# Graph attention: the edge weight's term moves from a TensorE product to VectorE's pass over the fetched rows

## The chip, the cores and the metric

One Trainium2 chip, one of its NeuronCores. The metric is the device time of one execution in microseconds (us); the kernel before was run three times. Engines are named as in the profile: PE (TensorE, with PEld for its weight loads), DVE (VectorE), ACT (ScalarE), POOL (GpSimd), SP (SyncE).

## The reference

A network of four graph layers over 6250 nodes with 128 features and 200000 edges sorted by target: a sum over neighbours, a message layer with a filter, an attention layer (GATv2) and a relation layer. The change concerns the attention layer alone:

```
h  = relu(layernorm(x))
xl = h @ Wl + bl ;  xr = h @ Wr + br
e  = edge_weight1 @ We                  # [200000, 1] @ [1, 128]
m  = leaky_relu(xl[src] + xr[dst] + e, 0.2)
logits = m @ att
ex     = exp(logits - segment_max(logits, dst)[dst])
out    = segment_sum(xl[src] * (ex / (segment_sum(ex, dst)[dst] + 1e-16)), dst) + bias_out
```

The edge weight is one number for each edge, so `e` is an outer product: weight of the edge times the row `We`.

## The kernel before, in words

**Edges and pairs.** The edges lie in groups of GE = 512 (KG = 4 sets of 128, one edge on each partition; edge 4p+q lies on partition p in set q). There are NGA = 392 groups. Target nodes lie in windows of 128. One step of the edge loops treats a *pair* of a group and a window that its edges reach; a group whose edges reach two windows stands in two successive pairs. There are NG = 440 steps. Lists made on the chip say which group (`pair_group`) and window (`pair_at`, `pair_window`) a step has; an engine reads them into a register and works out from it the slot of a buffer (`slot_of`).

**The stages.** The program first packs the edges into records of four words (weight, source, target, type: `pack_edges`), then has an edge loop for each layer with some node work between: sums, filter (`filter_messages`), a sum of messages, attention (`gat_edges`), relation (`relation`). Each is a block in which all engines have a program of their own, and all meet at its end.

**The attention loop, `gat_edges`.** `skewed` writes the software pipeline: each stage of an engine has a lead, in pairs, and the engine goes through its stages in the order given for one pair after another; `turn` is the number of pairs written out in the body of the loop (S = 8, U = 4). Engines wait on counting semaphores.

- SP: `load` brings a group's records into `rows` (16 slots), `weigh_in` its weights as 9 rows of bf16 into `weight` (8 slots), and `here`, `weighed_in`, `send`, `free` pass on what has landed or is free.
- POOL: `gather` issues four indirect DMAs (L2022) for a group, which fetch 512 rows of `xl` by source into `far`. This is done for the 392 groups, not for the 440 pairs.
- DVE, in this order: `meet` (L2062, near term plus far term), `bend` (L2074, leaky ReLU), `node_max` (L2082, L2084, L2086, the running maximum), `add` (L2094), `one_hots` (L2056), `columns` (L2050, targets relative to the window), `rows_to` (L2068, copies the fetched rows of a group from `far` to one of two buffers `far_s`).
- PE, in this order: `spreads` (L2176, L2177, L2179), `sums` (L2194), `spread_keys` (L2155), `rows_met`, `turn_prob` (L2185). In `rows_met` three products of the targets' rows with the one-hot matrix (L2168) and the product of `term` with the weight rows (L2169) go to one bank, and four transposes (L2171) turn `far_s`.
- ACT: copies out of PSUM (L2112, L2107, L2124), the exponentials (L2129, L2132), and L2118 and L2141.

The weight rows come from three bf16 parts: POOL splits the weights in `pack_edges` (`split_weights`), SP stores nine rows to memory (`store_weights`, L300) and waits for them at the end of the block (L351), and at the head of `gat_edges` DVE splits `We` likewise (L235 to L239) and builds `term` (L2035 to L2039), after it has cleared `weight` (L2032).

Of the kernel before, what the change touches and what calls it, by code (L numbers as in the profile page):

```python
# [12 lines left out]
BF16 = mybir.dt.bfloat16  # L13
# [66 lines left out]
def program(nc, x, src, dst, attr, etype, weight, W1, b1, W2, b2, W_in, W_f1, b_f1, W_f2, b_f2,  # L80
# [16 lines left out]
    with top:  # L97
# [7 lines left out]
        wrows = dram("weight_rows", [9, 2 * EP], BF16)  # L105
# [46 lines left out]
        def link(eng, ins):  # L152
# [11 lines left out]
        k.pair_lists, k.pair_bases, k.softs, k.wrows, k.gtable = pair_lists, pair_bases, softs, wrows, gtable  # L164
# [31 lines left out]
            "records_in", "weights_here", "rows_here", "rows_free", "weights_zeroed", "far_here", "far_taken", "marked", "product_ready", "message_turned")}  # L196
# [45 lines left out]
def pack_edges(k, kept):  # L242
# [17 lines left out]
    with ExitStack() as own:  # L260
# [3 lines left out]
        wt_rest = sb(own, "wt_rest", [P, J])  # L264
        wt_parts = [k.staging_t[:, :].bitcast(BF16)[:, 0:J], *(sb(own, f"wt_part{i}", [P, J], BF16) for i in (1, 2))]
# [19 lines left out]
        wt_split, wt_out = sem("wt_split"), sem("wt_out")  # L285

        def split_weights(eng, done):

            nc_eng = nc.gpsimd
            nc_eng.tensor_copy(wt_parts[0][:, :], e_wt[:, :]).then_inc(wt_split, 1)  # L290
            eng.wait_ge(wt_split, done + 1)
            nc_eng.tensor_tensor(wt_rest[:, :], e_wt[:, :], wt_parts[0][:, :], ALU.subtract).then_inc(wt_split, 1)
            eng.wait_ge(wt_split, done + 2)
            nc_eng.tensor_copy(wt_parts[1][:, :], wt_rest[:, :]).then_inc(wt_split, 1)
            eng.wait_ge(wt_split, done + 3)
            nc_eng.tensor_tensor(wt_parts[2][:, :], wt_rest[:, :], wt_parts[1][:, :], ALU.subtract).then_inc(wt_split, 1)

        def store_weights(eng, half):
            for r in range(9):
                eng.dma_start(k.wrows[r, half * EP:(half + 1) * EP].rearrange("(p j) -> p j", p=P), wt_parts[r % 3][:, :])\  # L300
                    .then_inc(wt_out, 16)
# [17 lines left out]
        with nc.Block() as block:  # L319
            @block.sync  # L320
            def _(sp):
# [25 lines left out]
                sp.wait_ge(wt_split, 4)  # L347
                store_weights(sp, 0)
                sp.wait_ge(rec_out, 48)
                sp.wait_ge(row_out, 16 * (NB + 1))  # L350
                sp.wait_ge(wt_out, 9 * 16)  # L351

            @block.gpsimd
            def _(pool):
# [25 lines left out]
                split_weights(pool, 0)  # L380
# [160 lines left out]
        earlier, owned, attr_out, wt_back, wt_free = sem("earlier"), sem("owned"), sem("attr_out"), sem("wt_back"), sem("wt_free")  # L541
# [5 lines left out]
        with nc.Block() as block:  # L547
# [43 lines left out]
            def _(sp):  # L591
                with if_mixed(sp):
# [18 lines left out]
                    with sp.Fori(0, NCH, 1) as c:  # L611
                        sp.wait_ge(wt_free, c + 1)
                        sp.dma_start(part[:, :, :].rearrange("p t c -> p (t c)"),
                                     k.erec[EP:2 * EP, :].rearrange("(p j) c -> p (j c)", p=P)[:, bass.ds(c * (T * RW), T * RW)])\
                            .then_inc(wt_back, 16)
                    sp.wait_ge(wt_split, 8)
                    store_weights(sp, 1)
                    sp.wait_ge(wt_out, 18 * 16)

            @block.gpsimd  # L620
            def _(pool):
                with if_mixed(pool):
# [12 lines left out]
                    pool.sem_inc(moved, 1)  # L635
                    pool.sem_inc(wt_free, 1)
                    with pool.Fori(0, NCH, 1) as c:
                        pool.wait_ge(wt_back, c * 16 + 16)
                        nc.gpsimd.tensor_copy(e_wt[:, bass.ds(c * T, T)], part[:, :, C_WT]).then_inc(wt_free, 1)
                    pool.wait_ge(wt_free, NCH + 1)  # L640
                    split_weights(pool, 4)


def scan(k, dve, source, n):

    cur, other = source, 0
    step = 1
# [1283 lines left out]
def gat_edges(k):  # L1931
# [16 lines left out]
    with ExitStack() as own:  # L1948
# [28 lines left out]
        with nc.Block() as block:  # L1977
            @block.sync
            def _(sp):
# [9 lines left out]
                def weigh_in(g, a):  # L1989
                    if isinstance(g, int) and a == 0:  # L1990
                        sp.wait_ge(k.stage["weights_zeroed"], 1)
# [753 lines left out]
```

## Time and profile before

| | us |
|---|---|
| median of three runs | 9282.66 (9282.63 to 9282.89) |
| profiled execution, its own time | 9295.66 |
| its span, first to last instruction | 9294.0 |
| PE busy (80% of the span) | 7420.9 |
| DVE busy (67%) | 6266.4 |
| POOL busy (67%) | 6250.4 |
| ACT busy (54%) | 5033.5 |
| attention loop, first to last L2084 | 4917.9 to 6993.3 |

The busy shares are means over stages with different limits. What the change is worth has to be read in the attention loop, at the head of it, and where the packing ends. A DVE instruction is shown with its start and its duration; durations of neighbours can overlap by some tens of nanoseconds, so the time that one takes in a row is the distance from start to start. "issue" is idle time of an engine in which the profile shows nothing that it waited for: its sequencer was at work on registers, addresses and waits.

### The profile page before, as it was taken

Reading aid. Unit: us, or ns where it says so; the run is one execution under the profiler, and the core shown is the slowest. Engines: PE = TensorE matmul, PEld = TensorE weight load, DVE = VectorE, ACT = ScalarE, POOL = GpSimd, SP = SyncE. Lnnn points to the kernel's source line nnn. Section 1 sums busy time; section 2 is a strip of 40 time slices with the busy share of each in tenths; the row PEclk is TensorE's granted clock in tenths of the full one; section 3 lists DMA queues with packets and bytes.
Section 4 is the critical chain, followed back from the end, with each engine's and each line's share of the span. In section 5 each row is a group of like instructions: output and inputs, shape, how many; then the busy total and the mean of one; then the engine's idle time right before and its main releaser. Section 6 shows DMA issues by size and latency. Waiting matters only on the chain. (4 is left out here: it accounts for less than half of the span.)

```text
span 9294.0 us, 257139 instructions
## 1 busy us (share of the span) xinstructions
PE 7420.9 (80%) x48775; PEld 5025.9 (54%) x49109; DVE 6266.4 (67%) x20821; ACT 5033.5 (54%) x11808; POOL 6250.4 (67%) x6542
## 2 busy tenths in 40 slices
PE   3699999996666666666978999999995777777777
PEld 2344455554333333335965666666663666666666
DVE  6577777776444455557976777777777666666666
ACT  4366666664333333332334555666665666666666
POOL 4777777772777777774217777777763766766664
PEclk7555555557888888888989999999998999999999
DMA  6355555553333344446842222222221222222221
GB/s 191 103 143 144 147 148 150 150 150 98 107 109 110 113 113 116 115 117 189 262 124 55 56 55 55 54 53 54 52 45 38 54 51 51 51 51 50 51 51 48
DMA packets 1004337, 900.19 MB, mean 97 GB/s; under 512 B 689602, under 2 KB 748099, under 8 KB 1003590
## 3 DMA queue, kind: packets, MB, share of 16 engines
q0 software_dynamic: 243504, 526.87, 21.2%
q10 hardware_dynamic: 309878, 260.87, 9.9%
q1 hardware_dynamic: 450592, 109.24, 5.4%
q14 instruction: 334, 2.74, 0.1%
q8 instruction: 29, 0.48, 0.0%
HBM read 663.38 MB, written 248.90 MB: 98 GB/s over the span
## 5 line engine op out<-in xcount | busy, mean ns | idle before, releaser
L2022 POOL DMA_INDIRECT a_far<-attention_table,a_rows x1568 | 1548.2, 987 | 657.9 <-issue 489.2
L1769 POOL DMA_INDIRECT message_records<-hs,f_pos x1564 | 1522.1, 973 | 622.9 <-issue 438.2
L2278 POOL DMA_INDIRECT r_far<-node_table,r_rows x1568 | 1488.7, 949 | 636.1 <-issue 452.2
L1377 POOL DMA_INDIRECT near<-split_table,t_rows x1568 | 1518.4, 968 | 482.1 <-issue 476.9
L1859 ACT ACTIVATE hs<-banks,f_rows 128x128 f32 x1760 | 503.1, 368 | 1200.6 <-DVE hs L1819 1084.5
L1565 PE MATMUL banks<-near,w_f 20*128 20x512 f32 x784 | 807.6, 1130 | 26.5 <-DVE list_store L1453 25.1
L1556 PE MATMUL banks<-near,t_hot 128*128 x5292 | 694.8, 304 | 167.0 <-SPq L1352 106.9
L1556 PEld LDWEIGHTS banks<-near,t_hot 128*128 128x128 bf16 x5292 | 586.1, 135 | 313.0 <-issue 228.3
L2129 ACT ACTIVATE list_store<-banks,staging 128x512 f32<-128x512 f32 x442 | 303.9, 688 | 819.6 <-DVE staging L2086 817.6
L1900 PE MATMUL banks<-f_hot_t,near 128*128 128x512 bf16 x1218 | 420.4, 458 | 357.3 <-DVE f_hot_t L1797 348.1
L1818 DVE COPY hs<-f_rows 128x12 int32 x441 | 84.7, 192 | 887.7 <-SPq L1753 884.6
L2417 PE MATMUL banks<-near,r_hot_t 128*128 x5328 | 621.7, 232 | 39.2 <-issue 1.9
L2194 PEld LDWEIGHTS banks<-a_far,a_prob 128*128 128x128 f32 x3528 | 431.1, 190 | 276.6 <-issue 276.6
L1904 PE MATMUL banks<-list_store,w_W_f 128*128 128x512 f32 x886 | 559.2, 719 | 0.0
L1890 PEld LDWEIGHTS banks<-ident_b,f_rel 128*128 128x128 bf16 x1780 | 131.4, 107 | 754.2 <-DVE f_rel L1791 648.2
L1462 DVE SCALAR_TENSOR_TENSOR near<-list_store,xs 128x512 f32<-128x512 f32 x392 | 268.3, 684 | 394.3 <-ACT xs L1514 374.4
L2444 PE MATMUL banks<-r_far,list_store 128*128 x3528 | 531.6, 296 | 0.0
L2382 ACT ACTIVATE list_store<-banks,r_prob 128x128 f32<-128x128 bf16 x1764 | 498.3, 364 | 40.0 <-PE banks L2428 27.3
L1573 PEld LDWEIGHTS banks<-ident,t_attr 128*20 128x20 f32 x1568 | 156.0, 120 | 642.2 <-issue 587.2
L2417 PEld LDWEIGHTS banks<-near,r_hot_t 128*128 128x128 bf16 x5328 | 432.2, 103 | 120.9 <-issue 98.3
L1679 PE MATMUL banks<-m_rows,m_hot 128*128 128x128 f32 x3528 | 434.9, 281 | 65.5 <-DVE m_hot L1640 45.6
L2194 PE MATMUL banks<-a_far,a_prob 128*128 x3528 | 476.3, 277 | 8.9 <-issue 3.9
(445 smaller groups left out, 19688.3 us busy)
## 6 DMA issues: line engine op xcount, KB each, us to landing
list_store<-soft_groups ACTq DMA_DIRECT2D x447, 256.0 KB
soft_groups<-near ACTq DMA_DIRECT2D x392, 256.0 KB
m_rows<-message_records SPq DMA_DIRECT2D x223, 264.0 KB
m_rows<-message_records POOLq DMA_DIRECT2D x223, 264.0 KB
near<-split_table,t_rows POOLq DMA_INDIRECT x1568
a_far<-attention_table,a_rows POOLq DMA_INDIRECT x1568
r_far<-node_table,r_rows POOLq DMA_INDIRECT x1568
message_records<-hs,f_pos POOLq DMA_INDIRECT x1564
```

What stands on the lines that cost most here:

```text
L1377: pool.indirect_dma_start(far[:, u * KG + q, :], None, k.table3[:, :], bass.IndirectOffsetOnAxis(ap=rows[:, u, q, C_SRC:C_SRC + 1].bitcast ...
L1556: last = nc.tensor.matmul(k.psum[a % 2][:, 0:D], hot[:, a % H, q, :], row[:, part * D:(part + 1) * D], start=q == 0 and part == 0, stop=q ...
L1565: nc.tensor.matmul(hidden_ps[a % 2], k.w_f1[:, :], attr_t[:, a % 2, :], start=True, stop=True).then_inc(hidden_ready, 1)
L1769: pool.indirect_dma_start(k.mrec[:, :], bass.IndirectOffsetOnAxis(ap=pos[:, u, q:q + 1], axis=0), msg[:, u * KG + q, :], None)\
L1859: last = nc.scalar.activation(msg[:, bass.ds(slot + q, 1), 0:D].rearrange("p a d -> p (a d)"), out_ps[b][:, q * D:(q + 1) * D], ACT.Copy, ...
L1904: nc.tensor.matmul(filter_ps[b], w_f2[:, :], soft[:, s, :], start=True, stop=True).then_inc(filter_ready, 1)
L2022: pool.indirect_dma_start(far[:, u, q, :], None, k.gtable[:, :], bass.IndirectOffsetOnAxis(ap=rows[:, a % R, q, C_SRC:C_SRC + 1].bitcast(I ...
L2194: last = nc.tensor.matmul(sum_ps[b][:, 0:D + 1], prob[:, b, q * P:(q + 1) * P], flat(far[:, slot, q, 0:D + 1]), start=q == 0, stop=q == KG ...
L2278: pool.indirect_dma_start(far[:, u, q, 0:D], None, k.table[:, :], bass.IndirectOffsetOnAxis(ap=rows[:, a % R, q, M_DST - M_SRC:M_DST - M_S ...
L2382: last = nc.scalar.activation(share[:, b, q, :], hot_ps[:, q * P:(q + 1) * P], ACT.Copy, scale=prob[:, u, q:q + 1])
L2417: nc.tensor.matmul(near_ps[b][:, span], hot_t[:, h, span], k.near[:, w, part * D:(part + 1) * D] .rearrange("p a d -> p (a d)"), start=par ...
L2444: last = nc.tensor.matmul(sum_ps[b][:, 0:D + 1], share[:, b, q, :], flat(far[:, slot, q, 0:D + 1]), start=q == 0, stop=q == KG - 1)
```

## The change

What it does, part by part:

1. `rows_to` no longer copies a group's 512 fetched rows with one instruction. It does four `scalar_tensor_tensor`, one for each set of 128: `far_s[q] = We * weight of the edge + far[q]`, where the weight is read from the record in `rows` by a pointer to one number for each partition. It therefore needs two slots, that in `far` (of 8) and that in `rows` (of 16).
2. PE's product L2169 goes, with its wait for `weights_here` and its slot.
3. SP's `weigh_in` and `weighed_in` go from the loop; `weight`, its clearing, `term`, `split3` of `We` and `which` go from the head of `gat_edges`.
4. `split_weights` and `store_weights` go from both blocks of `pack_edges` (the second runs only where the edges aren't sorted), with the wait for the stores.
5. The body of DVE's loop holds 4 pairs and not 8 (`turn=U`), and `rel` has 4 slots. PE and ACT keep 8.

```
-                sp.wait_ge(wt_split, 4)
-                store_weights(sp, 0)
                 sp.wait_ge(rec_out, 48)
                 sp.wait_ge(row_out, 16 * (NB + 1))
-                sp.wait_ge(wt_out, 9 * 16)
...
-                split_weights(pool, 0)
...
-                skewed(sp, (FREE, free), (LOAD, load), (HERE, here), (WEIGHT, weigh_in), (WEIGHED, weighed_in), (SENT, send), counts=now, turn=R, total=NGA, exact=True)
+                skewed(sp, (FREE, free), (LOAD, load), (HERE, here), (SENT, send), counts=now, turn=R, total=NGA, exact=True)
...
-                nc.vector.memset(weight[:, :, :], 0.0).then_inc(k.stage["weights_zeroed"], 1)
-                nc.vector.tensor_scalar(att[:, :], k.ones[:, :], k.att_col[:, :], None, ALU.mult)
-                split3(nc, link, split[0][:, :], split[1][:, :], split[2][:, :], We[:, :], left[:, :])
-                link(nc.vector.tensor_tensor(which[:, 0:3], k.ident[:, 0:9:3], k.ident[:, 1:9:3], ALU.add))
-                link(nc.vector.tensor_tensor(which[:, 0:3], which[:, 0:3], k.ident[:, 2:9:3], ALU.add))
-                link(nc.vector.tensor_scalar(term[:, :], split[0][:, :], which[:, 0:1], None, ALU.mult))
-                for i in (1, 2):
-                    link(nc.vector.scalar_tensor_tensor(term[:, :], split[i][:, :], which[:, i:i + 1], term[:, :], ALU.mult, ALU.add))
+                link(nc.vector.tensor_scalar(att[:, :], k.ones[:, :], k.att_col[:, :], None, ALU.mult))
...
                     wait(dve, now, near_ready, g, a, 2)
-                    nc.vector.tensor_copy(far_s[a % 2], far[:, bass.ds(slot_of(group), 1), :, 0:D].rearrange("p a q d -> p (a q) d"))\
-                        .then_inc(far_here, 1)
+                    slot, held = bass.ds(slot_of(group), 1), bass.ds(slot_of(group, R), 1)
+                    for q in range(KG):
+                        last = nc.vector.scalar_tensor_tensor(far_s[a % 2][:, q, :], We[:, :], flat(rows[:, held, q, C_WT:C_WT + 1]),
+                                                              flat(far[:, slot, q, 0:D]), ALU.mult, ALU.add)
+                    last.then_inc(far_here, 1)
...
-                skewed(dve, (SCORE, meet), (SCORE, bend), (MAX, node_max), (ADD, add), (HOT, one_hots), (COLS, columns), (HOT, rows_to), counts=now, turn=S)
+                skewed(dve, (SCORE, meet), (SCORE, bend), (MAX, node_max), (ADD, add), (HOT, one_hots), (COLS, columns), (HOT, rows_to), counts=now, turn=U)
...
-                    pe.wait_ge(weights_here, group)
                     wait(pe, now, far_here, g, a)
                     wait(pe, now, in1, g, a, 1)
                     wait(pe, now, onehotT_ready, g, a)
                     for i in range(3):
-                        nc.tensor.matmul(near_ps, flat(k.near[:, w, i * D:(i + 1) * D]), hot_t[:, a % H, :], start=i == 0, stop=False)
-                    nc.tensor.matmul(near_ps, term[:, :], weight[:, slot, :].rearrange("p a (e q) -> p (a q) e", q=KG), start=False, stop=True)
+                        nc.tensor.matmul(near_ps, flat(k.near[:, w, i * D:(i + 1) * D]), hot_t[:, a % H, :], start=i == 0, stop=i == 2)
```

## Rows read from the trace of the kernel before

**Rows 1.** The page: busy time of each engine over the span.
```profile
PE 7420.9 (80%) x48775; PEld 5025.9 (54%) x49109; DVE 6266.4 (67%) x20821; ACT 5033.5 (54%) x11808; POOL 6250.4 (67%) x6542
```

**Rows 2.** Stretches: attention early and late, filter; busy us, clock, DMA, GB/s.
```profile
core 0: us, PE busy (x) PEld busy (x) DVE busy (x) ACT busy (x) POOL busy (x), PEclk, DMA share, GB/s
4950.00:5320.00 370.00, 349.22 (x2075) 231.32 (x2112) 260.32 (x681) 206.05 (x526) 280.34 (x295) 1.00 0.26 56
6210.00:6580.00 370.00, 355.01 (x2200) 246.73 (x2240) 280.76 (x720) 226.00 (x559) 283.32 (x280) 1.00 0.25 53
2500.00:4200.00 1700.00, 1097.28 (x4819) 574.08 (x4911) 867.46 (x2268) 624.20 (x1890) 1294.12 (x1331) 0.85 0.40 113
```

**Rows 3.** One line's instructions: DVE's reduction (one a pair), POOL's gathers.
```profile
L2084 DVE TENSOR_REDUCE a_gmax<-banks x442: 672/679/684, 4917.9 to 6993.3; 128x1 f32<-128x512 f32 x148
```
```profile
L2022 POOL DMA_INDIRECT a_far<-attention_table,a_rows x1568: 941/947/1465, 4893.0 to 6947.4; - x196
```

**Rows 4.** Groups of 6210 to 6580 (80 pairs): busy, mean ns, idle before.
```profile
L2169 PE MATMUL banks<-a_weight,staging_t 128*128 x80 | 49.1, 614 | 0.0
...
L2062 DVE TENSOR_TENSOR staging_t<-banks,staging_t 128x512 f32<-128x512 f32 x80 | 55.3, 692 | 4.8
...
L2050 DVE TENSOR_SCALAR a_rel<-a_rows,list_store 128x4 f32 x80 | 20.1, 252 | 35.3 <-issue 32.2 <-SPq L1997 3.1
L2068 DVE COPY list_store<-a_far 128x512 f32 x40 | 17.4, 435 | 21.3 <-PE banks L2171 21.3
...
L2169 PEld LDWEIGHTS banks<-a_weight,staging_t 128*128 128x128 bf16 x80 | 7.6, 95 | 18.3 <-issue 18.3
```

**Rows 5.** Timeline of DVE, one pair of the attention loop: start, us.
```profile
6301.84 0.69 DVE L2062 TENSOR_TENSOR staging_t<-banks,staging_t 128x512 f32<-128x512 f32 x1
...
6304.40 0.35 DVE L2056 TENSOR_SCALAR a_hot_t<-a_keys,part_id 128x512 bf16<-128x512 bf16 x1
6305.17 0.23 DVE L2050 TENSOR_SCALAR a_rel<-a_rows,list_store 128x4 f32 x1 [0.43 <-issue]
6305.94 0.43 DVE L2068 COPY a_far_s<-a_far 128x512 f32 x1 [0.54 <-PE banks L2171]
6306.45 0.69 DVE L2062 TENSOR_TENSOR staging_t<-banks,staging_t 128x512 f32<-128x512 f32 x1
```

**Rows 6.** Timeline of DVE at the beginning of the attention loop.
```profile
4908.31 0.23 DVE L2050 TENSOR_SCALAR a_rel<-a_rows,list_store 128x4 f32 x1
4909.08 0.43 DVE L2068 COPY a_far_s<-a_far 128x512 f32 x1 [0.54 <-issue]
```

**Rows 7.** Timeline of DVE elsewhere: four, then two, short instructions in a row.
```profile
7011.24 1.12 DVE L2476 SCALAR_TENSOR_TENSOR hs<-acc,stat,hs 128x128 f32<-128x128 f32 x4
```
```profile
8006.20 0.29 DVE L2318 SCALAR_TENSOR_TENSOR r_work<-banks,r_far 128x128 f32<-128x128 f32 x1
...
8006.41 0.29 DVE L2318 SCALAR_TENSOR_TENSOR r_work<-banks,r_far 128x128 f32<-128x128 f32 x1
```

**Rows 8.** Timeline of DVE where a loop turns: attention, then relation.
```profile
6217.93 0.43 DVE L2068 COPY list_store<-a_far 128x512 f32 x1 [0.56 <-PE banks L2171]
6218.50 0.69 DVE L2062 TENSOR_TENSOR staging_t<-banks,staging_t 128x512 f32<-128x512 f32 x1
```
```profile
8017.35 0.35 DVE L2306 TENSOR_SCALAR r_hot_t<-r_keys,part_id 128x512 bf16<-128x512 bf16 x1 [3.65 <-PE banks L2428]
```

**Rows 9.** End of the first packing block: DVE's last instruction, SP's wait, SP's last stores.
```profile
114.61 0.21 DVE L530 TENSOR_TENSOR first<-scan,count 128x50 f32<-128x50 f32 x1
```
```profile
SPq L351 <- DMA weight_rows<-wt_part: 4.0, 1, 4.0
```
```profile
116.04 2.00 SPq L300 DMA_DIRECT2D weight_rows<-wt_part  x2
```

**Rows 10.** Timeline of DVE at the head of the attention block.
```profile
4890.04 1.76 DVE L2032 MEMSET a_weight<- 128x2048 uint32 x1 [1.68 <-PEq L1121]
...
4896.30 5.56 DVE L2040 MEMSET acc<- 128x6600 f32 x1 [1.44 <-issue]
```

More of the change, by code:

```diff
@@ L1943, in gat_edges @@
     wait, start = stages.wait, stages.start
-    records_in, rows_here, rows_free, weights_here = (k.stage[n] for n in ("records_in", "rows_here", "rows_free", "weights_here"))
+    records_in, rows_here, rows_free = (k.stage[n] for n in ("records_in", "rows_here", "rows_free"))
     We = k.wide["We"][0]
@@ L1949, in gat_edges @@
         sb = lambda name, shape, dt=F32: k.sb(own, "a_" + name, shape, dt)
-        rows, rel = sb("rows", [P, R, KG, RW]), sb("rel", [P, S, KG])
-        weight = sb("weight", [P, S, GE], BF16)
+        rows, rel = sb("rows", [P, R, KG, RW]), sb("rel", [P, U, KG])
         keys, hot_t = sb("keys", [P, 2, GE], BF16), sb("hot_t", [P, H, GE], BF16)
@@ L1955, in gat_edges @@
         prob_t = spare[:, GE:3 * GE].rearrange("p (b c) -> p b c", b=2)
-        att, term, left, *split = (k.staging_t[:, i * D:(i + 1) * D] for i in range(6))
-        term, split = term.bitcast(BF16)[:, 0:D], [t.bitcast(BF16)[:, 0:D] for t in split]
+        att = k.staging_t[:, 0:D]
         far_t = k.staging_t[:, 2 * D:6 * D]
         far_s = [t.rearrange("p (q d) -> p q d", d=D) for t in (spare[:, 0:GE], sb("far_s", [P, GE]))]
-        leaky, which = sb("leaky", [P, 2, GE]), sb("which", [P, 3])
+        leaky = sb("leaky", [P, 2, GE])
         gmax, before, bounded, factor = sb("gmax", [P, 1]), sb("before", [P, U]), sb("bounded", [P, U]), sb("factor", [P, U])
@@ L1967, in gat_edges @@
         flat = lambda t: t.rearrange("p a c -> p (a c)")
-        s_load, s_gather = [k.since(x) for x in loads_in], [k.since(x) for x in gathered]
+        s_gather = [k.since(x) for x in gathered]
         def slot_count(now, g, a, each, base=0):
@@ L1987, in load @@
                         .then_inc(k.rows_in[a % U], 16)
-                def weigh_in(g, a):
-                    if isinstance(g, int) and a == 0:
-                        sp.wait_ge(k.stage["weights_zeroed"], 1)
-                    u = a % S
-                    sp.dma_start(weight[0:9, u, :], k.wrows[:, bass.ds(moved + (g + a) * GE, GE)]).then_inc(loads_in[u], 16)
                 def here(g, a):
@@ L1997, in here @@
                     sp.sem_inc(records_in, 1)
-                def weighed_in(g, a):
-                    sp.wait_ge(loads_in[a % S], slot_count(now, g, a, 16, s_load[a % S]))
-                    sp.sem_inc(weights_here, 1)
                 def send(g, a):
@@ L2159, in rows_met @@
                 def rows_met(g, a):
-                    pair = pair_at(pe, k, o, g + a)
-                    w, group = window_in(k, pair), group_in(pair)
-                    slot = bass.ds(slot_of(group), 1)
-                    pe.wait_ge(weights_here, group)
+                    w = pair_window(pe, k, o, g + a)
                     wait(pe, now, far_here, g, a)
@@ L2199, in gat_edges @@
     for u in range(S):
-        k.since.passed(16 * len(range(u, NGA, S)), loads_in[u])
         k.since.passed(16 * KG * len(range(u, NGA, S)), gathered[u])
```

45 lines of the change are left out of this document (7 added, 38 removed).

## The prediction

> **What bounds the kernel now.** I read the page first. Its shares [rows 1] make PE look like the limit, at 80% of the span, with DVE and POOL both at 67%. They are means over stages, so I went to the stretches of the attention loop. There PE is busy 355.01 of 370 us late in the loop [rows 2], which still points to PE; but the late stretch holds 80 pairs, so a pair takes 370 / 80 = 4.625 us, and the question is how much of that each engine needs.
>
> The groups and the timeline of DVE answer for DVE. It is busy 280.76 / 80 = 3.51 us a pair [rows 2], which leaves 1.11 idle. Nearly all of that lies ahead of two short instructions: 35.3 / 80 = 0.44 before L2050 and 21.3 / 40 = 0.53 before L2068 [rows 4]. The first is called issue. The second is put down to PE's transposes L2171; the reader is to see that it isn't theirs. The distance from L2050's start to L2068's is 0.77 us in the running loop [rows 5], and also 0.77 at the loop's beginning, where the same gap of 0.54 is called issue [rows 6]. Both instructions follow a read of the list (`pair_group`) into a register, and each starts 0.77 after the one ahead of it. So this is the sequencer's own work, which the next instruction can't overlap. The only true slack of DVE is the 4.8 / 80 = 0.06 us ahead of L2062 [rows 4]. From L2062's start to L2068's there are 6305.94 - 6301.84 = 4.10 us [rows 5], and with the copy's 0.43 DVE can't go below 4.53 a pair. PE and DVE are both at the limit.
>
> POOL is the third. In the early stretch it issued 295 gathers in 370 us [rows 2], 1.254 us each or 5.02 for a group, and there it holds the pairs back; its 1568 gathers need 1966 us at least, and took 2054 [rows 3]. The loop took 6993.3 - 4917.9 = 2075.4 us from the first to the last L2084, over 441 distances [rows 3], 4.706 a pair. Late in the loop groups reach into two windows more often, pairs are more than groups, and PE and DVE rule.
>
> **The change, part by part.**
>
> *Four products in place of the copy.* The nearest rows: four `scalar_tensor_tensor` of 128x128 with a pointer scalar and all operands in SBUF take 1.12 us together [rows 7], and the last one's tail overlaps what follows it. In the relation loop a like instruction without a pointer, whose input also has a slot from a register, is 0.29 long and starts 0.21 after its neighbour [rows 7], so the tail is about 0.08, and one in the row costs (1.12 - 0.08) / 4 = 0.26. Lower end 0.21, upper end 1.12 / 4 = 0.28. I take 0.26, since that row has the pointer and the change has it too: four cost 1.04, where the copy took 0.43.
>
> *The second slot.* Ahead of the first product the sequencer works out one more slot, in `rows`. DVE shows no such step alone; PE does: its load for L2169 is preceded by 18.3 / 80 = 0.23 us of issue [rows 4], which is a slot and its address. I take 0.23, with 0 (hidden) and 0.46 (twice, as each of the four has two addresses) as ends.
>
> *The shorter body.* Where the attention loop turns, L2062 starts 0.57 after L2068 [rows 8]; behind the last product it would otherwise start after 0.26. The 0.31 is paid once in 4 pairs, 0.08 a pair. Today most of it hides in the copy's 0.43 and the slack, once in 8 pairs.
>
> *DVE's pace.* 4.10 + 0.23 + 1.04 + 0.08 = 5.45 us a pair. Nothing covers it: DVE had 0.06 of slack, and 5.45 is above POOL's 5.02 for a group too, so it holds in the early part as well, and with all pairs. The loop becomes 441 x 5.45 = 2403.5 us, 328.1 more. Ends: 4.10 + 0 + 0.84 + 0.08 = 5.02, and 4.10 + 0.46 + 1.12 + 0.08 = 5.76.
>
> A rule of the Trainium skill bears on the price of the four products. By "VectorE: DVE Perf Modes", section "The TRN2 errata", an SBUF-to-SBUF instruction of VectorE takes 58 cycles plus its elements at 0.96 GHz, so splitting a tile pays the fixed part each time, which speaks against this change. An estimate from it is 4 x 186 / 0.96 = 0.78 us, a pace of 5.19, and 9485 us. Rows 7 show more, 0.26 against 0.19 for each.
>
> *PE's product gone.* 49.1 / 80 = 0.61 us busy a pair and the 0.23 of issue [rows 4] go. It is worth nothing: PE would need about 4.2 of the 5.45, and waits for DVE. The transposes then wait for the products to end, some 0.8 later within DVE's turn than now, and the sum L2062 for that pair is a whole turn away, so this stays covered; if the cover were gone it would show as a gap ahead of L2062.
>
> *SP.* Two of its six stages go, with a DMA a group. SP isn't late in the loop: worth nothing.
>
> *Head of the attention block.* From the clearing of `weight` to that of `acc` there are 6.26 us [rows 10]; 0.2 for `att` and the 1.44 of issue ahead of `acc` stay, 4.6 go. All on DVE, which is now first to be late; ends 0 and 6.3.
>
> *End of the packing.* DVE is done at 114.8; SP's last two stores of weight rows are out at 118.0 and it waits 4.0 more for them to land [rows 9]. All engines meet there, so up to 118.0 + 4.0 - 114.8 = 7.2 us go. Other stores may still be landing, so I take 6.0, ends 0 and 7.2. POOL's split runs under DVE's work and is worth nothing.
>
> **The sum.** + 328.1 - 4.6 - 6.0 = + 317.5. The profiled execution took 9295.66 with a span of 9294.0, and becomes 9613; the median of the runs lies 13 lower, at 9282.66, so I say 9282.7 + 317.5 = 9600. DVE's two ends of pace give 9410 and 9737. What a measurement of this kernel can tell from no change is about 0.2%, 19 us.
>
> **The rivals.**
>
> *DVE's gap is a wait after all, and the products fill it (faster).* If the 0.53 ahead of L2068 waited for PE or for rows, as the view of groups says, losing L2169 would shorten it and the products would run where DVE now stands still. DVE would need 3.51 - 0.43 + 1.04 + 0.44 = 4.56 a pair in place of 4.625, 0.065 x 441 = 28 us, with the 10.6 of head and packing 9244; POOL's floor of 1966 allows no more than 88 + 10.6, 9184. The point that decides is a mean pace of 4.706 + 10.6 / 441 = 4.73. Against it stands the same 0.77 with nothing to wait for [rows 6]. Chance 0.07; 0.02 more that it lands within 0.2%.
>
> *The turn of the loop stalls.* In the relation loop DVE stands still 3.65 us once in eight pairs [rows 8], at the turn. Were that so here, once in four, a pair would cost 3.65 / 4 = 0.91 more: 6.36, and 10001 us. Against it: the attention loop of 8 pairs with 9 instructions of DVE each, 72, turns in 0.57, and the new body has 4 x 12 = 48. The Trainium skill, "Runtime: NRT & Kernel Launch", section "Instruction fetch mechanics", says that a branch to code which isn't held on the engine has to fetch it; by that rule the shorter body is what keeps the stall away. Chance 0.03.
>
> *PE's clock falls.* It is at 1.00 now; in the filter stage, with PE busy 1097.28 of 1700 us, 65%, it is 0.85 [rows 2], which is 1.2 GHz in 30% of the time. Here PE would be busy (355.01 / 80 - 0.61) / 5.45 = 70%. At 1.2 GHz its 3.83 us of work could double to 7.7, above DVE's pace, and 0.3 x (7.7 - 5.45) = 0.67 more a pair gives 6.12 and 9896. Against it: PE's idle time would come in short pieces, some 1.6 us in every pair. Chance 0.08.
>
> **How the numbers follow.** The forecast, DVE's pace between 5.0 and 5.8, has 0.80. The predicted time is its own, 9600. Its middle part, slot and pitch not at their ends together, is a pace of 5.18 to 5.76, 9480 to 9740; I leave out the low end, the faster rival and most of the two slow ones, together about 0.2. Faster 0.07, within 0.2% 0.02, slower 0.80 + 0.03 + 0.08 = 0.91.
>
> **What would show it right or wrong.** Right: in the attention loop four products start about 0.26 apart, the first some 1.0 after L2050's counterpart; no gap ahead of the sum; L2084's counterparts are 5.4 to 5.5 apart from first to last, early and late alike; POOL waits for free slots from early on; DVE's busy share in the loop is near (3.51 - 0.43 + 1.2) / 5.45 = 79%, PE's near 70%; the first gather of the program starts 6 us earlier. Wrong: pairs 4.6 or 5.0 apart (DVE hid the products, or POOL paces), a gap of some us once in four pairs, or a clock below 0.95 in the loop. The weakest term is the sequencer's: if each product waits for two addresses, all four cost more than 0.28; if the slot hides, the pace is nearer 5.2.

## The result, and the profile after

The changed kernel took 9567.72 us, the median of 4 runs (9563.87 to 9569.29), and the kernel before 9282.65, the median of 4 (9281.87 to 9282.89). The ratio is 1.0307, with a 95% interval of 1.0294 to 1.0320: slower by 285 us. Forecast were 9600 us, +317.5, in a range of 9480 to 9740, with 0.91 for slower. Mechanism and sign were right; the sum was 32 us too high, 9 of them in the loop that the change is in and 23 outside it.

From here DVE's old lines L2050, L2062, L2068 and L2084 are L1993, L2005, L2013 (four products where the copy was) and L2030, the gathers L2022 are L1972, and L505, L511 and L512 of the packing are L481, L487 and L488. First the page and the stretches of the kernel after, which answer to [rows 1, 2]:

```profile
PE 7373.3 (77%) x48331; PEld 4966.8 (52%) x48665; DVE 6539.4 (68%) x22145; ACT 4984.8 (52%) x11808; POOL 6214.0 (65%) x6538
```
```profile
4950.00:5320.00 370.00, 300.19 (x1805) 200.93 (x1840) 281.05 (x818) 185.07 (x479) 287.10 (x273) 1.00 0.23 50
6210.00:6580.00 370.00, 300.50 (x1807) 201.09 (x1842) 281.03 (x818) 185.02 (x480) 220.95 (x232) 1.00 0.20 43
```

The early and the late stretch are now alike in DVE, PE and ScalarE, which they were not before: one engine sets the pace throughout. Each stretch of 370 us holds 68 pairs (818 instructions of DVE, 12 a pair). DVE is busy only 76% of it, since a good part of what limits it is not busy time. PE's share is 81%, where 70% was forecast, and its clock is 1.00, so the rival with the falling clock is out.

The view of a line, after, answers to [rows 3]:

```profile
L2030 DVE TENSOR_REDUCE a_gmax<-banks x442: 677/680/691, 4889.4 to 7283.8; 128x1 f32<-128x512 f32 x148
```
```profile
L1972 POOL DMA_INDIRECT a_far<-attention_table,a_rows x1568: 938/944/1345, 4869.6 to 7228.1; - x196
```

From the first to the last reduction there are 7283.8 - 4889.4 = 2394.4 us, 319.0 more than before and 2394.4 / 441 = 5.43 a pair; 5.45 was forecast.

DVE's timeline, one pair, answers to [rows 5]:

```profile
6304.82 0.68 DVE L2005 TENSOR_TENSOR staging_t<-banks,staging_t 128x512 f32<-128x512 f32 x1
6305.54 0.69 DVE L2020 SCALAR_TENSOR_TENSOR a_leaky<-staging_t 128x512 f32<-128x512 f32 x1
...
6307.38 0.35 DVE L1999 TENSOR_SCALAR a_hot_t<-a_keys,part_id 128x512 bf16<-128x512 bf16 x1
6308.16 0.23 DVE L1993 TENSOR_SCALAR a_rel<-a_rows,list_store 128x4 f32 x1 [0.44 <-issue]
6309.16 1.14 DVE L2013 SCALAR_TENSOR_TENSOR list_store<-wide_We,a_rows,a_far 128x128 f32<-128x128 f32 x4 [0.76 <-issue]
6310.23 0.69 DVE L2005 TENSOR_TENSOR staging_t<-banks,staging_t 128x512 f32<-128x512 f32 x1
```

The reader is to see three things. From L2005 to the first product there are 6309.16 - 6304.82 = 4.34 us, where the sum had 4.10 + 0.23. The four products are 1.14 long together, with the next instruction 1.07 behind their start. And nothing stands ahead of L2005: both idle times of the pair are called issue, as are all but 4.7 us of those ahead of the two lines over the whole loop.

In the packing, DVE's count of the keys, L528 before and L504 after, moved by more than the forecast allowed:

```profile
112.52 0.21 DVE L528 COPY count<-banks 128x50 f32<-128x50 f32 x1 [0.75 <-PE banks L431]
```
```profile
103.43 0.21 DVE L504 COPY count<-banks 128x50 f32<-128x50 f32 x1 [0.75 <-PE banks L407]
```

DVE itself was done 9.1 us sooner. Nothing in the forecast had DVE's own work there get shorter. With DVE out of the way, the block now ends with SP, which waits for its last stores of the table's rows, issued up to 109.99:

```profile
SPq L328 <- DMA split_table<-near: 2.3, 1, 2.3
```

### The profile page after: what moved, and what is told of

The parts are those of the page before. It is cut to its first block and busy times, and to the rows that moved or that the text cites. A ratio compares the mean times of both kernels' runs of the same rounds, so it can differ in the third digit from the quotient of the medians.

```text
span 9567.3 us, 256120 instructions
## 1 busy us (share of the span) xinstructions
PE 7373.3 (77%) x48331; PEld 4966.8 (52%) x48665; DVE 6539.4 (68%) x22145; ACT 4984.8 (52%) x11808; POOL 6214.0 (65%) x6538
## 5 line engine op out<-in xcount | busy, mean ns | idle before, releaser
L1972 POOL DMA_INDIRECT a_far<-attention_table,a_rows x1568 | 1537.2, 980 | 973.4 <-issue 519.3
L1518 PE MATMUL banks<-near,t_hot 128*128 x5292 | 692.8, 305 | 164.1 <-SPq L1314 105.7
L2136 PE MATMUL banks<-a_far,a_prob 128*128 x3528 | 509.3, 287 | 79.4 <-issue 79.3
L2127 PE MATMUL banks<-ident,list_store 128*128 128x128 f32 x1768 | 290.3, 287 | 348.0 <-ACT list_store L2075 348.0
L2259 DVE SCALAR_TENSOR_TENSOR r_work<-banks,r_far 128x128 f32<-128x128 f32 x1772 | 413.9, 287 | 132.1 <-issue 99.8
```

Source lines behind the costliest of these rows:

```text
L1518: last = nc.tensor.matmul(k.psum[a % 2][:, 0:D], hot[:, a % H, q, :], row[:, part * D:(part + 1) * D], start=q == 0 and part == 0, stop=q ...
L1972: pool.indirect_dma_start(far[:, u, q, :], None, k.gtable[:, :], bass.IndirectOffsetOnAxis(ap=rows[:, a % R, q, C_SRC:C_SRC + 1].bitcast(I ...
L2136: last = nc.tensor.matmul(sum_ps[b][:, 0:D + 1], prob[:, b, q * P:(q + 1) * P], flat(far[:, slot, q, 0:D + 1]), start=q == 0, stop=q == KG ...
```

## The experiments

Twelve kernels ran. Seven stood beside runs of the kernel before with medians of 9280.3 us (the first four) and 9277.8 us (the last three):

| kernel | us, median | ratio to before, 95% | attention loop, us | relation loop, us |
|---|---|---|---|---|
| before | 9282.65 | | 2075.4 | 2133.2 |
| after | 9567.72 | 1.0294 to 1.0320 | 2394.4 | 2115.6 |
| e1_turn8 | 9639.91 | 1.0374 to 1.0409 | 2390.0 | 2192.8 |
| e2_before_turn4 | 9221.85 | 0.9923 to 0.9956 | 2071.3 | 2075.3 |
| e3_fixed_pointer | 9464.21 | 1.0182 to 1.0217 | 2317.1 | 2092.9 |
| e4_copy_no_term | 9227.25 | 0.9928 to 0.9961 | 2071.6 | 2099.7 |
| e10_order3 | 9307.41 | 1.0019 to 1.0042 | 2135.3 | 2116.9 |
| e11_order3_relation4 | 9160.28 | 0.9856 to 0.9889 | 2134.4 | 1967.2 |
| e12_before_both | 9161.62 | 0.9857 to 0.9889 | 2121.8 | 1969.1 |

The loops are the distances from the first to the last of 442 maxima over a pair, a_gmax and r_gmax, in the view of that line. The other five (e5, e6, e7, e9, e13) ran on another chip, called chip 8 below, where the four edge loops with POOL's indirect transfers took 25 to 46% longer and the kernel before 12174 to 12176 us. The sum of messages, a loop without such transfers, and the packing took what they did before (452.6 us for 451.9 from the first to the last L1602, in e9 and after). Something else than DVE's work sets the pace there: e5 and e6, which are the changed kernel but for a part of the packing, took 12196.85 and 12202.74 us against 12176.2, 0.2% more in place of 3.1%. So only durations, order and waits on an engine are read from these five.

**The four products and their slots.** Two kernels take the product's parts off one by one. e3 gives the four products a pointer that stands in a fixed place, so that no second slot is worked out (it leaves out the edge's weight and multiplies the row by the partition's number):

```
- flat(rows[:, held, q, C_WT:C_WT + 1])
+ k.part_id[:, 0:1]
```


> The changed kernel whose four products read their pointer scalar from a fixed column (the partition's number) and not from the record, so the slot in the records isn't worked out; it leaves out the edge weight and multiplies the row by that column. Theory, the slot is sequencer work ahead of the first product: the pace falls from 5.43 by 0.22 to 5.21 and the time by 97 us to 9470; the four products stay 0.26 apart. Rival, the slot is hidden or the products' own two addresses are the limit: the distance from the relative targets to the first product stays 1.0, or the products come closer together.

e4 has the old copy instead, and leaves the term out altogether, on PE as well:

```
- for q in range(KG): ... scalar_tensor_tensor(far_s[a % 2][:, q, :], We, ...)
+ nc.vector.tensor_copy(far_s[a % 2], far[:, slot, :, 0:D].rearrange(...))
```


> The changed kernel with the copy in place of the four products, and nothing of the edge weight's term on any engine: it leaves the term out. Theory, DVE sets the pace: without PE's product DVE needs 4.10 + 0.43 + 0.04 for the turn = 4.57 a pair late in the loop against 4.625 before, POOL 5.02 for a group early; 14 us less than before in the loop and 28 to 45 less outside it: 9225 to 9242. PE shows idle time in the late part. Rival, PE's product was what set the late pace, and DVE would follow: a late pace of 4.2 to 4.4 and about 9190.

Both came within 6 us of what was expected, e3 at 9464 for 9470 and e4 at 9227 for 9225 to 9242. The second slot is worth (2394.4 - 2317.1) / 441 = 0.18 us a pair, the products against the copy (2317.1 - 2071.6) / 441 = 0.56 over the loop. The latter is a mean that POOL holds down: early in e4's loop the gathers pace it, as before. e4 also says what PE's product for the term had cost: its loop is 2071.6 us and that of e2, which has the product, 2071.3. Nothing, as forecast. And DVE's two gaps stay with PE's product gone, as e4's timeline shows:

```profile
6305.19 0.23 DVE L1993 TENSOR_SCALAR a_rel<-a_rows,list_store 128x4 f32 x1 [0.43 <-issue]
6306.06 0.43 DVE L2012 COPY a_far_s<-a_far 128x512 f32 x1 [0.64 <-issue]
```

That it is sequencer work shows in the view of the line, where register operations stand as DVEq. Before, then after:

```profile
L2068 DVEq ALU_OP  x890: 45/45/45, 4907.2 to 6995.8; - x178
L2068 DVEq FUSED_REGOPS  x445: 57/57/65, 4907.4 to 6995.8; - x149
```
```profile
L2013 DVEq FUSED_REGOPS  x2225: 57/93/117, 4879.0 to 7287.0; - x186
L2013 DVEq ALU_OP  x1335: 40/45/45, 4878.8 to 7286.5; - x191
...
  issue: 349.7, 441
```

The 445 pairs had two operations and a fused one ahead of the copy. Now they have three and five fused. One more operation, of 0.04 us, and one more fused one, of 0.07 in the pair shown, stand ahead of the first product; from the first of these operations to DVE's instruction the trace has 0.25 us in the pair of [rows 5] and 0.47 now. The other three fused ones go with the products behind it, whose distance stayed at 0.26. The last row is DVE's idle time ahead of L2013 that nothing but issue ends: 0.79 us a pair.

**Does the length of DVE's body matter?** Two kernels change it alone, the attention loop's of the changed kernel back to eight pairs, and that of the kernel before to four:

```
- skewed(dve, ..., (HOT, rows_to), counts=now, turn=U)    # after: 4
+ skewed(dve, ..., (HOT, rows_to), counts=now, turn=S)    # e1: 8, e2 the other way
```


> The changed kernel with DVE's body written out for eight pairs again (and eight slots of the relative targets). Theory, DVE's own work sets the pace of 5.43 us and a turn costs 0.31 us: paid once in eight pairs, it saves 0.04 a pair, 17 us, so about 9550, pace 5.39. Rival, a body this long stalls at its turn as the relation loop's does (3.65 us before): about 0.4 a pair more, 9720 to 9740, with one gap of 3 to 4 us in every eight pairs ahead of DVE's sum of near and far term. The body has 96 DVE instructions, between the 72 that turned without a stall and the relation loop's 168, so I hold both for equally likely.

> The kernel before with DVE's body of four pairs and nothing else of the change. Theory: the shorter body costs a turn (0.57 in place of at most 0.51 from the copy to the sum) once in four pairs and not in eight, at most 0.03 a pair and only late in the loop where DVE and PE set the pace: 9283 to 9292. Rival, the 285 us come from the shorter body and not from the products: 9500 or more.

In the attention loop the body's length is worth 2394.4 - 2390.0 = 4.4 us and 2075.4 - 2071.3 = 4.1 us: neither a stall nor a gain. Once in four against once in eight was to cost 0.04 a pair, half of the forecast's 0.08, and costs 0.01. Both times moved all the same, and neither lies where it was expected, e1's by 72 us up and e2's by 58 down, and that happened in the relation loop, whose source neither touches: 77 us longer and 58 shorter. Its DVE stands still once in eight pairs, at the turn [rows 8], and by how much differs from build to build. After and e1, timeline of DVE there:

```profile
8033.74 0.35 DVE L2247 TENSOR_SCALAR r_hot_t<-r_keys,part_id 128x512 bf16<-128x512 bf16 x1 [2.96 <-ACT r_keys L2301]
```
```profile
8008.30 0.35 DVE L2247 TENSOR_SCALAR r_hot_t<-r_keys,part_id 128x512 bf16<-128x512 bf16 x1 [3.14 <-ACT r_keys L2301]
...
8010.41 0.35 DVE L2288 SCALAR_TENSOR_TENSOR r_cur<-r_cur,r_factor,banks 128x129 f32<-128x129 f32 x1 [1.48 <-issue]
```

The second kernel has a second standstill, of 1.48 us, right behind the first; it comes in 51 of the 55 turns and makes 77 us. In the seven kernels of the table whose relation loop has eight pairs, the interval with the turn lasts from 7.5 (e2) to 9.5 us (e1) on average and every other one 4.1 to 4.7.

**The relation loop's turn.** e9 and e11 give that loop a body of four pairs, with its rings cut from eight slots to four:

```
- u, f = a % S, bass.ds(g + a, 1)          # and likewise in each ring
+ u, f = a % U, bass.ds(g + a, 1)
- skewed(dve, ..., (COLS, columns), counts=now, turn=S)
+ skewed(dve, ..., (COLS, columns), counts=now, turn=U)
```


> The changed kernel with VectorE's relation loop turned every four pairs and not every eight (its rings cut from eight slots to four; nothing is left out); the attention loop is untouched. It measures what the once-per-turn standstill of the relation loop is worth, which moved by itself between the kernels so far (relation loop 2136 us before, 2118 after, 2078 and 2196 in the two runs with another body length in the attention loop). Theory (the loop's first instructions have to be fetched again when the body is long, as in the relation loop's 8 pairs, and not when it is short): intervals of 4.1 to 4.7 us throughout and no 8.1 us one, relation loop 1880 to 1960 us, time 9330 to 9410 us. Rival (a standstill of the same size comes at each turn, so twice as often): relation loop 2300 us or more, time over 9750 us. Second rival (the shorter rings make VectorE wait for TensorE): no standstill, but intervals over 4.8 us, time 9500 to 9600 us.

e9 fell on chip 8 (12205.13 us against 12176.2) and decides nothing. e11, below, repeats it on top of e10: relation loop 2116.9 to 1967.2, time 9307.41 to 9160.28, 7 and 10 us above the ranges expected. In the whole loop DVE has no idle time over 1.3 us left, where e10 has 56. So the long body pays about 2.7 us a turn, net, and the short one nothing of the kind. Body and rings were shortened together, and no run has one without the other. The Trainium skill, "Runtime: NRT & Kernel Launch", section "Instruction fetch mechanics", says that a branch back to code outside the stretch held on the engine waits for a fetch. The runs agree in that the two attention bodies, of four and of eight pairs, turn freely and the longer relation body doesn't; what moves the amount from build to build wasn't tried by itself, so that it is the code's place is only argued.

**The packing.** Each of the two parts that the change removed from the packing was put back alone, POOL's four split instructions (e5) and nine stores of the same size by SP, of a tile that is there anyway (e6). The tiles have 128x1570 elements, not the 128x785 that the two expectations say:

```
+ nc.gpsimd.tensor_copy(wt_parts[0][:, :], e_wt[:, :]) ... # e5, and three more on POOL
```
```
+ for r in range(9):                                        # e6
+     sp.dma_start(k.wrows[r, 0:EP]..., win[0][:, :]).then_inc(wt_out, 16)
+ sp.wait_ge(wt_out, 9 * 16)
```


> The changed kernel with one removed part put back: POOL splits the 128x785 weights in three in the first packing block (its four instructions, nothing stored). Theory: POOL's instructions on large tiles slow VectorE's instructions that run at the same time, so VectorE's cast on L511's line goes from 0.43 to about 1.6 us, the subtraction after it from 0.69 to about 3.5 us, and the packing block ends 6 to 9 us later; the first gather of relation-free stages moves from 121.7 to 128 to 131 us, and the time from 9568 to 9574 to 9577 us. Rival, the prediction's own term (POOL's split is hidden and worth nothing): VectorE's durations stay 0.43 and 0.69 us, first gather 121.7 to 122.5, time 9568 us within the noise of the relation loop (20 us).

> The changed kernel with the other removed part of the packing block put back: nine stores of one tile of 128x785 bf16 into a table that nobody reads, issued by SP at the end of the first packing block, with the wait for them; nothing is split. Prediction's term: stores and their wait end the block 6.0 us later, first gather at 127.7 us. Theory after the traces: SP's stores run beside VectorE's and SP's other work, VectorE's end sets the block's, and the stores alone cost 0.5 to 2 us: first gather at 122 to 124 us. Either way the time stays within 9560 to 9580 us, so the verdict is read from the start of the first gather, not from the time.

Timeline of DVE with the split (before, one line, then e5), then without (after); POOL's first two split instructions in e5 are the last fence:

```profile
55.17 3.52 DVE L512 TENSOR_TENSOR near<-x_rest,near 128x512 bf16<-128x512 f32 x1
```
```profile
53.37 1.60 DVE L497 CAST near<-x_rest 128x512 bf16<-128x512 f32 x1
55.01 3.52 DVE L498 TENSOR_TENSOR near<-x_rest,near 128x512 bf16<-128x512 f32 x1
58.45 1.85 DVE L491 TENSOR_SCALAR win_halves<-win_halves 128x1570 bf16<-128x1570 bf16 x1
```
```profile
53.44 0.43 DVE L487 CAST near<-x_rest 128x512 bf16<-128x512 f32 x1
53.91 0.69 DVE L488 TENSOR_TENSOR near<-x_rest,near 128x512 bf16<-128x512 f32 x1
54.51 1.04 DVE L481 TENSOR_SCALAR win_halves<-win_halves 128x1570 bf16<-128x1570 bf16 x2
```
```profile
52.74 1.95 POOL L360 CAST staging_t<-e_wt 128x1570 bf16<-128x1570 f32 x1
54.78 3.20 POOL L362 TENSOR_TENSOR wt_rest<-e_wt,staging_t 128x1570 f32<-128x1570 f32 x1
```

A cast of 0.43 us takes 1.60 and a subtraction of 0.69 takes 3.52: each ends 0.3 to 0.6 us after the POOL instruction that runs beside it (54.97 against 54.69, 58.53 against 57.98). DVE isn't slowed in proportion, it is held until POOL has finished. With the split DVE's count came at 112.08, without it (e9, same chip) at 103.49. The Trainium skill says this in "SBUF — State Buffer", section "SBUF: two separate sides": the port pair that VectorE and GpSimd share is a lock, which an instruction that needs it (of VectorE: one in a two-port mode, or with two inputs in SBUF) has until it ends. The two durations agree with that. By that rule the forecast should have priced the split.

The stores, alone, left DVE where it was (count at 103.55) and held the block's end: SP waited 4.7 us for them, and POOL's first gather came at 129.32 us against 120.35 in e9, 9.0 later. My expectation of 0.5 to 2 us was wrong. The split, alone, moved DVE's count by 8.6 us but the first gather only to 123.77, 3.4 later, where I had expected 6 to 9: without the stores the block ends with whichever is later, DVE (done at 114.4 in e5) or SP's stores of rows (landed at 109.99 + 2.3 = 112.3 in the changed kernel). So the two parts overlap. In the kernel before the stores of weights, landed at 122.0, covered DVE's 114.8; with the stores alone gone DVE would be the end, 7.2 us sooner, and only with the split gone too does the end move the last 2.5. One start is good to some us only: in the nine kernels of the table the first gather comes at 129.2 to 131.0 with both parts and at 119.2 to 122.1 without, and e7, with e9's packing, began at 125.49, its count 4.7 us late as well.

**The order of DVE's stages.** If a slot costs what the instruction ahead of it doesn't cover, a long instruction ahead of it should hide it. e7 puts the products behind the sum:

```
- (SCORE, meet), (SCORE, bend), (MAX, node_max), (ADD, add), (HOT, one_hots), (COLS, columns), (HOT, rows_to)
+ (SCORE, meet), (HOT, rows_to), (SCORE, bend), (COLS, columns), (MAX, node_max), (ADD, add), (HOT, one_hots)
```


> The changed kernel with VectorE's stages in another order: the sum with the near rows, then the four products, then the leaky step, the keys' subtraction, the running maximum, the addition and the one-hot test. Nothing is left out. Theory (what a pair costs on VectorE is not its 4.3 us of busy time but the idle 0.77 and 0.75 us in which its sequencer loads and computes two register slots behind short instructions): with the register work behind the 0.65 us sum and the 0.6 us leaky step, the pace falls from 5.43 to 4.6 to 4.9 us, the loop by 230 to 365 us, the time to 9200 to 9340 us. Rival (the pair is bound by the length of VectorE's instructions or by the chain through TensorE, and the order is immaterial): pace 5.35 to 5.5 us, 9540 to 9600 us. Second rival (the products in front wait for the gathered rows or for TensorE's turning of the pair before): VectorE's idle time in front of the products ends in a semaphore, pace over 5.5 us.

e7 fell on chip 8 as well (12164.21 against 12176.2 us), but its DVE timeline answers, in a stretch where no transfer was late:

```profile
8002.90 0.69 DVE L2005 TENSOR_TENSOR staging_t<-banks,staging_t 128x512 f32<-128x512 f32 x1 [1.55 <-ACT staging_t L2058]
8003.98 1.14 DVE L2013 SCALAR_TENSOR_TENSOR list_store<-wide_We,a_rows,a_far 128x128 f32<-128x128 f32 x4 [0.38 <-issue]
8005.03 0.68 DVE L2020 SCALAR_TENSOR_TENSOR a_leaky<-staging_t 128x512 f32<-128x512 f32 x1
8005.64 0.22 DVE L1993 TENSOR_SCALAR a_rel<-a_rows,list_store 128x4 f32 x1
...
8006.61 0.16 DVE L2032 SCALAR_TENSOR_TENSOR staging<-a_gmax,a_bounded 128x1 f32<-128x1 f32 x1
...
8008.88 0.69 DVE L2005 TENSOR_TENSOR staging_t<-banks,staging_t 128x512 f32<-128x512 f32 x1 [1.53 <-ACT staging_t L2058]
```

The gap ahead of the products fell from 0.76 to 0.38 and that ahead of L1993 went. But the pair grew to 8008.88 - 8002.90 = 5.98 us: from the start of L2032, whose end lets ScalarE go on, DVE has only 0.7 us of work left before the next sum, and ScalarE needs 2.2 until its copy for that sum is there. It was the wait that took the gap's place. In this loop 278 of 442 pairs are 5.9 to 6.1 us apart and none less than 5.7; in e9, with the old order on the same chip, the commonest are 5.4 and 5.5. The 4.6 to 4.9 expected didn't come. e10 keeps the products in that place and moves only the keys' subtraction behind the sum and the one-hot test behind the products:

```
+ (SCORE, meet), (COLS, columns), (SCORE, bend), (MAX, node_max), (ADD, add), (HOT, rows_to), (HOT, one_hots)
```


> The changed kernel with VectorE's attention stages in a third order: the sum with the near rows, the keys' subtraction, the leaky step, the running maximum, the addition, the four products, the one-hot test. Nothing is left out. The order with the products straight behind the sum (e7_order) closed the idle time ahead of them from 0.75 to 0.38 us and ahead of the keys' subtraction from 0.38 to nothing, but put only 0.8 us of work between the maximum's last step and the next sum, while ScalarE's four instructions after that step and its copy of the far rows take 2.2 us, so VectorE then waited 1.5 us for ScalarE. Here the four products (idle time and all 1.7 us) stand in that place again. Theory (a slot's register work costs what the instruction ahead of it doesn't cover): keys' subtraction covered by the 0.69 us sum, products 0.65 us behind the 0.35 us addition: 0.70 + 0.13 + 0.60 + 0.12 + 0.72 + 0.13 + 0.98 + 1.05 + 0.35 = 4.8 us a pair, the loop 280 us shorter than the changed kernel's, the time 9270 to 9310 us on a chip that gives the kernel before 9283 us. Rival (register work costs its 1 us wherever it stands): 5.3 to 5.45 us a pair, 9510 to 9575 us. Second rival (VectorE waits for ScalarE here too): idle time in front of the sum, ended by ScalarE, pace over 5 us.

9307.41 us, in the range expected and 260 less than the changed kernel, for the same instructions. DVE's idle time ahead of L1993 and L2013, views of the two lines, after and then e10:

```profile
  issue: 194.2, 442
```
```profile
  issue: 2.2, 3
  SPq L1951: 0.5, 1
```
```profile
  PE banks L2113: 215.4, 316
  SPq L1955: 77.6, 78
  issue: 35.1, 51
```

The 194.2 us ahead of the keys' subtraction are gone; ahead of the products 349.7 + 3.3 became 215.4 + 77.6 + 35.1 = 328.1, since the 0.35 us addition covers little. The name PE is again that of whatever came last by the profile: with it as with issue the gap is 0.6 to 0.8 us nearly each time. The 78 under SPq L1955, which passes on that gathered rows have landed, are 1.0 us in the median and lie mostly in the early half; there POOL's gathers hold DVE in part.

**Both kernels at their best.** e11 is e10 with the relation loop's short body. e12 is the kernel before with short bodies in both loops and e10's order, the copy where e10 has the products:

> e10_order3 with VectorE's relation loop turned every four pairs (rings of four). Nothing is left out. Against e10_order3 it gives the relation loop's once-per-turn standstill alone, on a chip whose DMA is not the limit. Theory (a long body has to be fetched again at its turn, a short one doesn't): no interval of 8 us left, relation loop 1880 to 1960 us instead of 2080 to 2200, time 9040 to 9150 us. Rival (a standstill at each turn, twice as often): relation loop over 2300 us, 9500 us or more. Second rival (rings of four make VectorE wait for TensorE): intervals over 4.8 us throughout, time about that of e10_order3.

> The kernel before with the same three things: attention body of four pairs, VectorE's stages in e10_order3's order (its copy of the fetched rows in the place of the four products), relation body of four pairs. TensorE's product for the weight, the weight rows and their loads are all in. It tells what the change itself is worth once VectorE's register work is covered. Theory (the copy's slot is loaded behind the addition, the keys' subtraction is covered, TensorE at some 4.3 us a pair comes next): attention pace 4.3 to 4.5 us against 4.63, time 8900 to 9000 us, still 150 us or more ahead of e11_order3_relation4, because 1.05 us of products stand against a copy of 0.37 us. Rival (without the weight's product on TensorE the changed kernel is the faster of the two): over 9100 us.

They took 9160.28 and 9161.62 us, both 1.3% ahead of the kernel before and over 400 us ahead of the changed one, and the change is worth nothing between them: 12.6 us more in the attention loop, and 14 less outside it. I expected e12 to take 8900 to 9000 us and to lead by 150. It doesn't, because in it the copy is too short for the place, as the view of its L2062 shows:

```profile
L2062 DVE TENSOR_TENSOR staging_t<-banks,staging_t x443: 670/691/694, 4897.6 to 7023.9; 128x512 f32<-128x512 f32 x148
its engine sat idle before it (us, times) until:
  ACT staging_t L2112: 210.7, 374
```

The sum waits 210.7 us in all, 0.48 a pair, for ScalarE's copy, where e10's products fill the time: 2121.8 against 2134.4 us of loop. e12's order made its loop 50 us longer than the 2071.3 of e2. The last kernel was to give the kernel before its own order and both short bodies:

```
- skewed(dve, (HOT, one_hots), ..., (COLS, columns), counts=now, turn=S)   # relation, e2 plus e9's edit
+ skewed(dve, (HOT, one_hots), ..., (COLS, columns), counts=now, turn=U)
```


> The kernel before with its own order of VectorE's attention stages, and both of VectorE's bodies of four pairs (attention and relation). Nothing is left out and TensorE's product for the weight is in. It tells whether the change is worth anything when each kernel has the order that suits it: e11_order3_relation4, the changed kernel at its best, took 9160 us. Theory (in the kernel before the order was not what was short: 4.63 us a pair in e2_before_turn4 against 4.77 in e12_before_both, where the sum waited 0.5 us for ScalarE): attention loop 2071 us, relation loop 1970 us, so 9222 less 2078 plus 1970: 9105 to 9125 us, some 45 us ahead of e11. Rival (the relation loop's gain belongs to the attention loop's other order, by where the code comes to lie): relation loop over 2050 us, 9190 us or more.

It fell on chip 8, 12196.94 against 12174.39 us. Whether the kernel before, at its best, is ahead of e11 stays open; 9221.85 - 2075.3 + 1968 = 9115 would be the estimate.

## Why the prediction was right, point by point

- **What bounds the loop.** Right. DVE's chain of starts sets the pair, and the two gaps, which the groups put down to PE's transposes in part [rows 4], are the sequencer's. e4 and the two orders show it from two sides: with PE's product gone both stay (0.43 and 0.64 us); with a longer instruction ahead the first goes (e7, e10) and the second halves (0.76 to 0.38 in e7).
- **Four products.** Forecast 4 x 0.26 = 1.04; measured 1.05 to 1.07 to the next start. The 0.78 that the lower estimate had for the four, and its 9485 us, didn't come.
- **The second slot.** Forecast 0.23, from a row of PE's; measured 0.24 by distance (4.34 against 4.10) and 0.18 by leaving it out.
- **The turn.** 0.08 forecast; the half of it that e1 can tell, 0.04, measured 0.01. This term was too high and the products' a little too low, so that 5.45 for 5.43 is in part luck.
- **The loop.** +328.1 forecast, +319.0 measured.
- **PE's product and SP's stages worth nothing.** Right, by e4 against e2, and with PE's clock at 1.00. But PE is busy 300.50 / 68.2 = 4.41 us a pair and not 3.83, hence the 81%: the product's 0.61 can't be taken off a busy time of 4.44 in which records overlap. The rival with the clock was worked out from the 3.83; at 4.41 its loss would have been larger.
- **Head of the block.** -4.6 forecast. The first gather of the stage came 4893.0 - 4869.6 = 23.4 us sooner and the first reduction 4917.9 - 4889.4 = 28.5, so the head gave 5.1; against e2, which has the old head, it gave 4.6.
- **The packing.** The step that failed is "POOL's split runs under DVE's work and is worth nothing". It held DVE for 8.6 us, and the 7.2 us that the forecast took as the most that could go were counted to DVE's old end, 114.8. DVE ended at 105.7, SP's stores of rows became the end, and the block's first gather came 131.04 - 121.67 = 9.4 us sooner, not 6.0.
- **What the sum had no term for.** Outside the loop the profiled executions differ by 273.3 - 319.0 = -45.7 us, where -10.6 was forecast: 9.4 in the packing, 14.0 from there to the attention stage's first gather, 5.1 in the head, and 17.2 behind the loop, all of that in the relation loop (2133.2 to 2115.6), by a smaller standstill at its turns, which by the second experiment is a thing of the build. The 14.0 are hardly the change's: the execution profiled of before lay 13.0 above its median, that of after 1.6, and e2, with before's code up to there, reached the attention loop's first reduction 12.3 us sooner than it, at 4905.6. Against e2 the changed kernel is 4905.6 - 4889.4 = 16.2 us sooner there, and 319.0 - 16.2 - 17.6 = 285.2 us is what the medians say too (285.1). By this count the 32 us that the forecast was too high are 9 in the attention loop, 6 in packing and head and 18 in the relation loop, where it had no term.
- **The rivals.** None came: no wait that the products filled, no stall at the attention loop's turn, no fall of the clock. POOL waits for free slots from early on: 273 gathers in the early stretch in place of 295 [rows 2], and 303.0 us of waiting ahead of its gathers in place of 17.6.

## What to carry to other kernels

Where an engine's idle time is called issue ahead of a short instruction with an address from a register, price the register work as a span from the start of the instruction ahead, here some 1.0 us for two slots and 0.77 for one, and put a long instruction there; it was worth 260 us here, nearly the whole loss of the change. But before moving stages, count what the order leaves between the instruction that frees the next engine and the one that needs its answer: ScalarE's 2.2 us made the pairs of e7's better-looking order longer than those of the one it replaced. And when a time moves, look first whether the moved time lies in the loop that was edited.

## What the runs showed of the hardware that I had not expected

- DVE is held, not slowed, beside POOL's large instructions: 0.69 us became 3.52 beside one of 3.20. How much of that reaches the end of a block is another matter: 3.4 of 8.6 us in e5.
- The same relation loop, with the same source, took 2075.3 to 2192.8 us in seven kernels with a body of eight pairs, nearly all by what DVE stands still at its 55 turns; with a body of four it took 1967.2 and 1969.1. An edit in another loop gained 58 us (e2) and lost 77 us (e1) in that way, 0.6 and 0.8% of the kernel, more than the interval of a comparison.
- Chips differ: the same kernel before took 9278 to 9283 us in three sets of runs, on two other chips at least, and 12174 to 12176 in two sets on chip 8, with VectorE's instruction durations in the attention loop unchanged. The change cost 285 us in the first set, and on chip 8, with a part of the packing put back, 21 and 27 (e5, e6). The loops that took longer there are those with POOL's indirect transfers; why, no run settles.
